# A POOL/DVE exchange and new turn orders in the mixing stage of a decoder layer kernel

## What is computed

```python
paths = jnp.stack([_dwconv(v, fir_s).reshape(b, Ln, H, DV), _dwconv(v, fir_m).reshape(b, Ln, H, DV), _dwconv(v, fir_l).reshape(b, Ln, H, DV), delta_path, v.reshape(b, Ln, H, DV)], axis=3)
stats_flat = jnp.concatenate([_stats(paths[..., p, :]) for p in range(P)], -1)
gate_in = jnp.concatenate([hs, stats_flat], -1)
logits = jax.nn.gelu(gate_in @ gW1 + gb1, approximate=False) @ gW2 + gb2
...
o = jnp.einsum('blhp,blhpd->blhd', probs, paths)
o = o * jax.lax.rsqrt(jnp.mean(o * o, -1, keepdims=True) + 1e-05) * norm_w
return o.reshape(b, Ln, D) @ Wo
```

## Time and profile before

| | |
|---|---|
| time, median of 3 runs | 1570.22 us (1565.67 to 1572.8) |
| profiled execution: its own time | 1569.91 us |
| profiled execution: span | 1568.2 us |
| mean granted TensorE clock, share of full | 0.937 |
| mixing stage on PE: first and last matmul | 326.69 us to about 667.6 us |
| busy share of the span: PE, DVE, ACT, POOL | 86%, 58%, 44%, 35% |

### The profile page before, as it was taken

How to read it: one execution, slowest core, us unless ns; L and a number is a source line. 1 busy time by engine, 2 the same in 40 slices (tenths; PEclk the granted TensorE clock), 3 DMA queues, 4 the chain that set the end, 5 groups by cost and what they waited for, 6 DMA issues and landing times. The chain is left out here.

```text
span 1568.2 us, 24828 instructions
## 1 busy us (share of the span) xinstructions
PE 1355.5 (86%) x8188; PEld 1035.6 (66%) x8189; DVE 915.1 (58%) x1735; ACT 689.8 (44%) x1253; POOL 541.7 (35%) x460
## 2 busy tenths in 40 slices
PE   4889556669999999569999999969979999999995
PEld 1344456658888888358888888855756666666653
DVE  4899759769999999535454445446512212122196
ACT  2545349947777777323433343331022222222214
POOL 2565500014555555522312331211234444444311
PEclk9999878889999999679999999979989999999998
DMA  3698787744333332042232021023021111111164
GB/s 89 149 244 234 207 221 198 216 121 104 95 94 94 94 94 61 14 123 71 85 98 98 31 62 61 28 81 110 0 74 54 57 57 55 56 56 57 59 200 134
DMA packets 147325, 158.20 MB, mean 101 GB/s; under 512 B 63440, under 2 KB 112176, under 8 KB 145712
## 3 DMA queue, kind: packets, MB, share of 16 engines
q1 hardware_dynamic: 134320, 123.63, 27.0%
q0 software_dynamic: 8320, 29.37, 7.3%
q10 hardware_dynamic: 4608, 4.20, 0.8%
HBM read 104.72 MB, written 42.99 MB: 94 GB/s over the span
## 5 line engine op out<-in xcount | busy, mean ns | idle before, releaser
L2531 DVE TENSOR_TENSOR hidden<-unit_psum,gate 128x352 f32<-128x352 f32 x72 | 37.8, 525 | 210.1 <-ACT gate L2494 210.1
L1944 POOL TENSOR_TENSOR scores<-scores,score_max 128x1024 f32<-128x1024 f32 x32 | 60.8, 1899 | 243.2 <-DVE score_max L1872 243.2
L478 PE MATMUL proj_psum<-filtered 128*128 128x512 f32 x192 | 96.0, 648 | 34.8 <-DMA filtered<-in_xT 28.1
L2462 PE MATMUL unit_psum<-wd,hiddenT 128*128 (+1 forms) x432 | 112.0, 395 | 14.2 <-issue 12.9
L549 PE MATMUL proj_psum<-window,toep 128*128 128x128 f32 x512 | 77.2, 319 | 46.8 <-DMA toep<-in_fir 24.3
L2393 POOL DMA_INDIRECT unit_rows<-x_rows,token_of_slot x72 | 69.8, 970 | 126.9 <-PE unit_psum L2436 104.4
L668 ACT ACTIVATE filtered<-proj_psum 32x512 f32<-32x512 f32 x168 | 98.6, 587 | 30.3 <-PE proj_psum L549 26.3
L549 PEld LDWEIGHTS proj_psum<-window,toep 128*128 128x128 f32 x512 | 73.4, 231 | 50.5 <-issue 47.6
L697 DVE SCALAR_TENSOR_TENSOR filtered<-proj_psum,conv_taps,filtered 128x508 f32<-128x508 f32 (+1 forms) x144 | 95.0, 733 | 19.3 <-ACT filtered L596 19.3
L2400 POOL DMA_INDIRECT outs<-unit_out,choice_of_slot x72 | 71.1, 987 | 99.8 <-DVE unit_out L2536 97.1
L2462 PEld LDWEIGHTS unit_psum<-wd,hiddenT 128*128 128x128 f32 (+1 forms) x432 | 76.4, 190 | 37.0 <-issue 29.1
(11 more groups left out here) (286 smaller groups left out, 3258.5 us busy)
## 6 DMA issues: line engine op xcount, KB each, us to landing
toep<-in_fir SPq DMA_DIRECT2D x32, 384.0 KB, 4.0
neg_decay_blocks<-in_gw1s POOLq DMA_DIRECT2D x8, 1280.0 KB, 10.6
ndg<-filtered SPq DMA_DIRECT2D x8, 1024.0 KB, 6.1
neg_decay_gram<-ndg SPq DMA_DIRECT2D x16, 512.0 KB, 3.7
ctxT_tiles<-in_ctxT SPq DMA_DIRECT2D x16, 512.0 KB, 3.6
gathered<-outs SPq DMA_DIRECT2D x32, 256.0 KB, 3.0
window<-value SPq DMA_DIRECT2D x32, 192.0 KB, 4.0
filtered<-in_xT SPq DMA_DIRECT2D x8, 512.0 KB, 7.0
```

Source lines behind the costliest of these rows:

```text
L478: mm = pe.matmul(psum[:, pair_bank(n, p, m % 2), :], wqkv[m // KD][:, k, (m % KD) * 128:(m % KD) * 128 + 128], xT[:, u, k, :], start=(k == ...
L1944: pool.tensor_tensor(sc[:, i % 2, t, :, :], sc[:, i % 2, t, :, :], wide(mx[:, t, :], [128, XH, L], 2), ALU.subtract).then_inc(shifted[t], 1)
L2462: mm = pe.matmul(psum[:, u, DOWN, 0:D], hidT[0:HR[t], u, t, :], M.wd[0:HR[t], bass.ds(chosen["down"], 1), t, :].rearrange("p e n -> p (e n)"),
```

## The change

In words:

- The addition of the delta path (`add_delta`) and the scaling of the mixed tile (`scale_mix`) go from DVE to POOL. `scale_mix` then stands right behind `mix_inverse` on POOL.
- `path_sums` becomes one step for both tiles; the value sums are one reduction over both tiles for each kind of sum, so 2 in place of 4 for an item. The filter sums stay 4.
- `path_sums` and `delta_sums` signal their own ends, and PE's `statsT` waits for both.
- The lists of all five engines are in another order, with other lags.

```diff
-            staged_pair_loop(sp, PAIRS, (load_solver, 1), (load_keys, 1), (load_gate, 1), (load_x, 3), (load_grams, 0))
+            staged_pair_loop(sp, PAIRS, (load_gate, 2), (load_x, 4), (load_solver, 1), (load_keys, 1), (load_grams, 0))
...
+                pe.wait_ge(path_sums_made, i + 1)
+                pe.wait_ge(delta_sums_made, i + 1)
                 pe.wait_ge(norms_made, i + 1)
...
-                    if m == 0:
+                    if m == 2:
                         pe.wait_ge(gate_in, 16 * (i + 1))
...
-            staged_pair_loop(pe, PAIRS, (solve_rows(0), 1), (hidden_x(2), 2), (hidden_x(3), 2), (solve_rows(1), 1),
-                             (mixedT, 4), (output, 4), (statsT, 2), (scores, 1), (hidden_stats(0), 2), (solve_rows(2), 1),
-                             (hidden_stats(1), 2), (solve_rows(3), 1), (logits, 2), (hidden_x(0), 1), (delta_rows, 1),
-                             (cross_blocks, 0), (hidden_x(1), 1))
+            staged_pair_loop(pe, PAIRS, (solve_rows(0), 1), (hidden_x(0), 2), (solve_rows(1), 1), (mixedT, 4),
+                             (hidden_x(1), 2), (statsT, 2), (solve_rows(2), 1), (hidden_stats(0), 2), (output, 4), (hidden_stats(1), 2),
+                             (scores, 1), (solve_rows(3), 1), (logits, 2), (hidden_x(2), 1), (delta_rows, 1), (cross_blocks, 0),
+                             (hidden_x(3), 1))
...
-            staged_pair_loop(act, PAIRS, (square_delta, 1), (keep_cross, 0), (keep_rows(0), 0), (copy_mixed, 3), (norms, 1),
-                             (keep_rows(1), 0), (copy_stats, 1), (gelu(0), 1), (keep_rows(2), 0), (gelu(1), 1),
-                             (keep_rows(3), 0), (normalize, 3), (square_mix, 2), (exps, 1), (square_paths, 0))
+            staged_pair_loop(act, PAIRS, (square_mix, 3), (square_delta, 1), (keep_cross, 0), (keep_rows(0), 0),
+                             (norms, 1), (keep_rows(1), 0), (copy_mixed, 3), (copy_stats, 1), (square_paths, 0), (gelu(0), 1),
+                             (keep_rows(2), 0), (gelu(1), 1), (keep_rows(3), 0), (exps, 1), (normalize, 3))
...
+                val = M.value[:, :, :, pairs(j, u)].rearrange("p (h k) c b -> p b h (k c)", k=HK)
+                for s, mag in ((0, False), (2, True)):
+                    for t in range(P):
+                        ins = dve.tensor_reduce(stat[:, u, t, 0:12, s], filtered_heads(M, tile(j, u, t)), AX.XY, ALU.add,
+                                                apply_absolute_value=mag)
+                    ins = dve.tensor_reduce(stat[:, u, :, 16:20, s], val, AX.X, ALU.add, apply_absolute_value=mag)
+                ins.then_inc(path_sums_made, 1)
...
-                dve.wait_ge(mix_step, i + 1)
-                dve.tensor_tensor(mixed[:, :, :], mixed[:, :, :], delta[:, u, :, :], ALU.add).then_inc(mix_summed, 1)
...
-            staged_pair_loop(dve, PAIRS, (residual, 4), (sum_paths, 3), (ln_shift, 4), (mask_scores, 1), (path_sums(1), 0),
-                             (shift_logits, 2), (mix_norm, 3), (probabilities, 2), (scale_delta, 1), (scale_mix, 3),
-                             (delta_sums, 1), (square_sums, 1), (path_sums(0), 0))
+            staged_pair_loop(dve, PAIRS, (delta_sums, 1), (path_sums, 0), (residual, 3), (sum_paths, 2),
+                             (mask_scores, 0), (shift_logits, 1), (ln_shift, 3), (probabilities, 1), (scale_delta, 0), (mix_norm, 2),
+                             (square_sums, 0))
...
+            def add_delta(j, u):
+                i = 2 * j + u
+                pool.wait_ge(mix_step, i + 1)
+                pool.tensor_tensor(mixed[:, :, :], mixed[:, :, :], delta[:, u, :, :], ALU.add).then_inc(mix_summed, 1)
+
+            def scale_mix(j, u):
+                i = 2 * j + u
+                pool.wait_ge(mix_power, i + 1)
+                own = mixed[:, :, :].rearrange("p b (h d) -> p (b h) d", d=DV)
+                pool.tensor_tensor(own, own, wide(mix_r[:, :], [128, P * H, DV], 2), ALU.mult).then_inc(mix_scaled, 1)
...
-            staged_pair_loop(pool, PAIRS, (ln_inverse, 4), (make_rhs, 0), (mix_inverse, 3), (weight, 2))
+            staged_pair_loop(pool, PAIRS, (make_rhs, 0), (mix_inverse, 3), (scale_mix, 3), (weight, 2), (ln_inverse, 3),
+                             (add_delta, 2))
```

More of the change, by code:

```diff
@@ L938, in mix_paths @@
         ssq_made = signal("squares_summed")
+        path_sums_made = signal("path_sums_made")
+        delta_sums_made = signal("delta_sums_made")
         norms_made = signal("norms_made")
@@ L1278, in scale_delta, with path_sums @@
                                   ALU.mult).then_inc(delta_kept, 1)
-            def path_sums(t):
-                def step(j, u):
-                    i = 2 * j + u
-                    if not is_early(j, u, 2):
-                        dve.wait_ge(statsT_mm, i - 1)
-                    fir, val = filtered_heads(M, tile(j, u, t)), value_heads(M, tile(j, u, t))
-                    for s, mag in ((0, False), (2, True)):
-                        dve.tensor_reduce(stat[:, u, t, 0:12, s], fir, AX.XY, ALU.add, apply_absolute_value=mag)
-                        dve.tensor_reduce(stat[:, u, t, 16:20, s], val, AX.XY, ALU.add, apply_absolute_value=mag)
-                return step
+            def path_sums(j, u):
+                i = 2 * j + u
+                if not is_early(j, u, 2):
+                    dve.wait_ge(statsT_mm, i - 1)
+                val = M.value[:, :, :, pairs(j, u)].rearrange("p (h k) c b -> p b h (k c)", k=HK)
[5 more added lines that the diff above has]
+                ins.then_inc(path_sums_made, 1)
             def delta_sums(j, u):
@@ L1296, in delta_sums @@
                 for s, mag in ((0, False), (2, True)):
-                    dve.tensor_reduce(stat[:, u, :, 12:16, s], delta[:, u, :, :].rearrange("p b (h d) -> p b h d", d=DV),
-                                      AX.X, ALU.add, apply_absolute_value=mag)
+                    ins = dve.tensor_reduce(stat[:, u, :, 12:16, s], delta[:, u, :, :].rearrange("p b (h d) -> p b h d", d=DV),
+                                            AX.X, ALU.add, apply_absolute_value=mag)
+                ins.then_inc(delta_sums_made, 1)
             def square_sums(j, u):
@@ L1360, in mix_norm @@
                 dve.tensor_scalar(mean_sq[:, 1, :], mean_sq[:, 0, :], 1.0 / DV, 1e-5, ALU.mult, ALU.add).then_inc(mean_made, 1)
-            def scale_mix(j, u):
-                i = 2 * j + u
-                dve.wait_ge(mix_power, i + 1)
-                own = heads(mixed[:, :, :].rearrange("p b w -> p (b w)"))
-                dve.tensor_tensor(own, own, wide(mix_r[:, :], [128, P * H, DV], 2), ALU.mult).then_inc(mix_scaled, 1)
             def residual(j, u):
```

## The result

| | before | after |
|---|---|---|
| median of 12 runs | 1570.18 us (1565.67 to 1574.56) | 1578.36 us (1574.17 to 1583.76) |
| ratio, 95% interval | | 1.0053 (1.0036 to 1.0069) |
| profiled execution: its own time | 1569.91 us | 1580.98 us |
| profiled execution: span | 1568.2 us | 1579.3 us |
| mean granted TensorE clock | 0.937 | 0.929 |

The change makes the kernel 8.2 us slower, 0.5%. The profiled execution of after is 2.6 us above its median. It is under the lowest of the 12 runs, and the two together tell what is steady and what comes and goes.

A forecast was written before the change was run, and what follows sets the result against it. PE's own work, 18.94 us a turn plus a 0.73 stall, was taken to set the loop, DVE nearly full. From 1569.9: -8.8 stall, +0.5 `statsT` waits, +4.5 ramp, +3.8 end, +2.0 clock gives 1572, range 1563 to 1580.

The forecast's parts named there:

- rival A: The forecast itself: loop turns at about 18.95 us, the gain given back at both ends; 1568 to 1577, chance 0.55.
- The stall before `output`: PE's 0.73 us a turn waiting for ACT's copy goes in 12 turns, covered by four pieces: 8.8 us gained.
- Does a wait take its place?: Layout of one loop turn at 18.94 us: all slacks small but positive, 0.5 before `mixedT`, so the full 8.8 taken.
- DVE's spare 1.0: DVE needs 17.9 us a loop turn, leaving 1.0, said to hold small gate operations' waits behind POOL, about 0.4.
- Test (1) of the forecast: Loop turns of 18.9 to 19.0 us, no idle before `output`, DVE busy about 18; turns over 19.2 refute it.
- POOL's prices: Addition and scaling on POOL taken at 1.27 us each; POOL's turn grows from 10.94 to 13.5, not the bound.
- Rival C: Slower: `scale_mix` on POOL late before `mixedT`, by slow scaling or DVE's small operations waiting; 1579 us, chance 0.16.
- The ramp's stalls: In turns 1 to 3 `solve_rows(3)` waits for ACT behind `square_paths`: 1.1, 1.7 and 1.7, sum 4.5 us.
- rival D: Slower: the clock falls in ramp and end, costing 3 and 4.8 us; 1575.7 to 1578, chance 0.08.
- The end: From turn 16 on, `mixedT` of item 13 waits for POOL's scaling, making item 15's `weight` 5.1 late: +3.8 us.
- The clock term: At the end PE idles 2.9 us, so its clock may fall earlier: 2 us taken, bounds 0 and 4.8.
- rival B: Faster: the loop gain comes and the ends give little back; 1565.8, or 1561.6 with none; chance 0.17.

The follow-up runs named there:

- changed_again: The changed kernel, unedited, profiled once more in one execution: 1570.09 us, beside 1570.9 of the kernel before.
- rhs_before_add: The changed kernel with POOL's `make_rhs` moved ahead of `ln_inverse`, away from DVE's small operations: 1569.5 us.
- ramp_squares_last: The changed kernel with `square_paths` back at the end of ACT's turns 0 to 2: 1569.4 us.
- new_order_dve_add_scale: The changed kernel's new orders, but with the addition and the scaling back on DVE: 1600.08 us.

## Why the prediction came out as it did

1572 was forecast, with 1563 to 1580 around it; 1578.4 was measured. The forecast called everything over 1578 slower, with a chance of 0.22, and gave 0.62 to no change. The measured time lies 0.4 over that line and over rival A's own 1568 to 1577, and the interval of its ratio (5.7 to 10.8 us slower) has that line inside it. By its own steps:

- **The stall before `output`, right.** It is gone in every turn, under the four pieces of cover. -8.8 was its worth as long as nothing took its place.
- **"Does a wait take its place?", wrong.** The answer was no. `mixedT` waits about 0.3 in 7 of 12 turns (in 10 of `changed_again`), and most turns take about 19.17 where the same pieces without a wait take 18.45 (`rhs_before_add`): 0.7 lost. Another 0.2 of it stands before `delta_rows` (1.16 from the start at 532.22 to that at 533.38, where `rhs_before_add` has 0.95). The step that failed is the sentence that the small operations' delays (about 0.4 a turn) "stay within DVE's spare 1.0". The size was near: 0.60 on `ln_shift` and 0.21 on the subtraction of the logits. But DVE's spare time was the wrong cover. `ln_shift` stands on a chain over ACT, DVE and POOL to `mixedT` whose slack I had put at 0.5 in the same part, and never charged with it. `rhs_before_add` showed it: without the overlap 8.9 us come back. There POOL is done scaling (538.71 + 1.04 = 539.75) 0.78 before `mixedT` starts; counted from the start of the turn, after's tile is ready 1.1 later.
- **It stayed hidden in the sum, because another term erred the other way.** PE's own work is not 18.94 a turn but 18.45. Differences of starts on PE depend on the neighbour: `mixedT` costs 0.50 (521.86 to 522.36) where it had 0.66 and then a wait; `hidden_stats` 0.97 (524.54 to 525.51) for 1.06; `output` 1.73 (525.51 to 527.24) for 1.83. The lost 0.7 brings it back to 19.17, and the first turns of the loop are shorter (18.44 and 18.63 in `changed_again`), so without a fall the loop gained 7.3 for the forecast 8.3. Test (1) of the forecast, turns of 18.9 to 19.0, failed: most turns take 19.1 to 19.2, at the edge of what was to refute it. That the loop came out near its forecast is luck: two errors of 0.5 and 0.7 a turn nearly cancelled.
- **POOL's prices.** The scaling costs 1.04, not 1.27; the addition 1.27 as taken. Rival C named the right place, `scale_mix` before `mixedT`, with the wrong cause ahead of its right one: the scaling is fast, and the small operations' wait, its last sentence, acts from less than the 1.0 a turn that it asked for.
- **The ramp's stalls, right.** 1.01, 1.65 and 1.67 by the profile, 4.3 for 4.5. **The ramp's clock, missed.** Turn 3 is 6.5 longer than turn 2 with the same stall. The sum had no term for it; rival D priced it at 3, with 0.08. This is the largest part of the miss: the ramp cost 10.3 and 10.2 in the two profiles, for 4.5.
- **The end.** 66.6 and 64.0 for 65.5 plus 2.0 of clock; +5.0 and +2.4 for +5.8. The waits of its mechanism are there: `mixedT` of item 13 waits 3.08 for POOL's scaling, forecast 2.9, and the first `weight` of item 15 begins 41.4 after the start of turn 16 (658.25 - 616.81) in after and 38.6 in `changed_again`, forecast 39.8. The clock term is not steady: it came in one profile and not in the other, as the rows below show.
- **The value sums** cost 1.06, and **DVE** 18.1 a turn (181.47 in ten), for 1.1 and 17.9.
- **The chances.** "Faster" got 0.16, nearly the whole 0.17 of rival B, though B's own sum, 1565.8, is not faster. That number did not follow from the rivals.

The end of after, on PE and on POOL:

```profile
638.41 0.66 PE L1142 MATMUL mix_psum<-ident,mixed 128*128 128x128 f32 x4 [3.08 <-POOL mixed L1442]
638.91 1.73 PE L1107 MATMUL mix_psum<-xT_tiles,gate_w_x 128*128 128x256 f32 x4
...
658.25 0.61 POOL L1428 TENSOR_TENSOR delta_path<-delta_path,gate_exps 128x256 f32<-128x256 f32 x1
```

The same two pieces of PE in `changed_again`:

```profile
630.10 0.66 PE L1142 MATMUL mix_psum<-ident,mixed 128*128 128x128 f32 x4 [3.08 <-POOL mixed L1442]
630.60 1.03 PE L1107 MATMUL mix_psum<-xT_tiles,gate_w_x 128*128 128x256 f32 x4
```

Behind the same wait of 3.08 the four matmuls take 1.73 in after, where the clock has fallen, and 1.03 in `changed_again`, as at full clock in the loop. There it falls only some 8 us later, near the end of the logits.

So the forecast's +2.0 missed 6.2. The ramp, with the clock that the sum had no term for, makes 5.7 of it in either profile; the loop is 1.0 worse without a fall and 5.7 with the two of after, and the end is 0.8 to 3.4 better than forecast. What stays open: why the clock falls in some turns of the loop. It was seen in three profiles of the new orders with waits of PE in the loop (two in after, one in `ramp_squares_last`, five in `new_order_dve_add_scale`), in none of the three of the new orders without (but for one wait of 0.3 in turn 4 of two of them), but also not in `changed_again`, nor in any of the old orders, some of which wait 0.7 a turn. No run told what sets it off.

## What to carry to other kernels

Before an operation goes to POOL, list the small operations of DVE that read two SBUF tensors beside it, and charge each with the rest of POOL's instruction on every chain it stands on, not on DVE's total; moving POOL's operation by two places in its order undid the cost here. A step of an order that is hidden in the full turn must be looked at in the turns of the ramp, where the pieces that hid it are missing, and a stall there is to be charged with the clock behind it, which here cost more than the stall. Where two engines are full at once, relieve both in the smallest edits first: the exchange and a swap of two pieces in the old order gave what the whole new plan gave at its best.

## What the runs showed of the hardware

- A DVE operation of two elements took 0.75 us beside a product on POOL and 0.15 without; one of 40 elements 0.41 and 0.20.
- A stall of 1.67 us, the third in three turns, was followed within 0.2 us by some 13 us at a granted clock of 0.50, with PE busy all the while; 6.5 us lost. A single wait of 3.08 us at the end was followed by such a fall in one profile of the kernel and not in the other.
- POOL scales 512 fp32 elements by a value repeated over 64 of them in 1.04 us, and adds two dense tensors of 512 in 1.27.
- A sum over 512 elements 128 bytes apart costs DVE 1.06 us, over 512 dense ones 0.68:

```profile
L1294 DVE TENSOR_REDUCE path_stats<-value 128x8 f32 x12 | 12.8, 1063 | 0.0
L1301 DVE TENSOR_REDUCE path_stats<-delta_path 128x8 f32<-128x512 f32 x15 | 9.6, 678 | 0.0
```
